# Four-block vision tower: fifth passes of the experts' first layer in row halves, and the second layer in parts between groups of four tiles

## The reference, cut to what matters

```python
h = tok_ref(x)                          # patches to 8 x 64 tokens of 192, a ViT block
h = _layernorm(h + _L0_attn_ref(h))     # 4 experts of windowed attention, gated
h = _layernorm(h + _L0_ffn_ref(h))      # 8 experts, 192 -> 768 -> 192: here
h = _layernorm(h + _L1_attn_ref(h))
h = _layernorm(h + _L1_ffn_ref(h))      # m0: 192 -> 768 -> 192, and class experts: here

def _L0_ffn_ref(x, ...):
    ...
    topv, topi = jax.lax.top_k(probs, 2)
    comb = jnp.sum(topv[..., None] * one_hot(topi, E), axis=2)
    h = gelu(einsum('bnd,edf->bnef', x, w1) + b1)
    y = einsum('bnef,efd->bned', h, w2) + b2
    ffn_out = einsum('bne,bned->bnd', comb, y)
    return ffn_out + bk_scale * spec_out      # spec_out: two recurrences over 64 tokens
```

## Time and profile before

| | us |
|---|---|
| runs | 402.53, 399.41, 400.3 |
| median | 400.3 |
| profiled execution | 399.92 |
| its span (first to last instruction) | 398.2 |
| TensorE busy with matmuls in the span | 377.0 |
| VectorE, ScalarE, GpSimd busy | 242.2, 172.5, 69.3 |

### The profile page before, as it was taken

One profiled execution on the slowest core, in us unless ns is written; L12 is line 12 of the kernel. 1 busy time (PEld: TensorE's weight loads), 2 busy tenths in 40 slices (PEclk: granted clock), 3 DMA queues, 4 the chain that ended last, 5 costly groups with the idle time before them and its releaser, 6 DMA issues.

```text
span 398.2 us, 8780 instructions
## 1 busy us (share of the span) xinstructions
PE 377.0 (95%) x3602; PEld 310.4 (78%) x3602; DVE 242.2 (61%) x712; ACT 172.5 (43%) x302; POOL 69.3 (17%) x113
## 2 busy tenths in 40 slices
PE   8999899999899899989999899999999999999993
PEld 7988779779567575676577698899899898788783
DVE  1567756813299897996364577557658208676443
ACT  1255543471455666644524806325324411541420
POOL 7140010430013231432010400000000200304003
PEclk9999999999999999999999999999999999989999
DMA  8999900000249600000008984404411000000001
GB/s 198 263 203 211 193 17 2 1 2 0 50 124 299 160 2 2 3 2 2 2 0 211 267 210 128 137 10 132 140 21 39 2 0 2 2 2 2 0 2 40
DMA packets 28725, 30.69 MB, mean 77 GB/s; under 512 B 4867, under 2 KB 24137, under 8 KB 28686
## 3 DMA queue, kind: packets, MB, share of 16 engines
q1 hardware_dynamic: 28220, 29.96, 30.4%
q10 hardware_dynamic: 306, 0.17, 0.2%
q0 software_dynamic: 160, 0.01, 0.0%
HBM read 29.73 MB, written 0.39 MB: 76 GB/s over the span
## 4 chain that ended last, share of the span: by engine, by line
PE 62%; DVE 16%; issue 6%; SPq 5%; DMA 5%; ACT 3%; POOL 2%; DVEq 0%; POOLq 0%
PE ps L1533 57%; PE ps L1537 4%; SPq L360 4%; DMA wide<-in_w 3%; DVE front L1204 2%; DMA front<-in_x 2%; DVE front L1193 2%; DVE front L1182 1%; POOL rstd L529 1%; DVE bn L1034 1%; PE ps L1545 1%; DVE front L1194 1%; DVE xn L1049 1%; DVE front L1184 1%; DVE front L1205 1%
## 5 line engine op out<-in xcount | busy, mean ns | idle before, releaser
L1533 PE MATMUL ps<-halves 128*128 128x512 f32 (+2 forms) x380 | 84.4, 376 | 1.7 <-ACT front L747 1.7
L1533 PEld LDWEIGHTS ps<-halves 128*128 128x128 f32 x380 | 66.4, 188 | 14.2 <-ACT front L747 2.6
L1533 PE MATMUL ps<-wide,front 128*128 128x192 f32 x432 | 72.0, 327 | 0.0
L1533 PEld LDWEIGHTS ps<-wide,front 128*128 128x128 f32 x432 | 70.4, 190 | 1.0 <-issue 0.5
L1533 PEld LDWEIGHTS ps<-front 64*32 64x32 f32 (+3 forms) x1488 | 51.4, 132 | 20.5 <-issue 9.4
L1533 PE MATMUL ps<-front 64*32 64x64 f32 (+3 forms) x1488 | 60.0, 241 | 5.8 <-issue 2.3
L747 ACT ACTIVATE front<-ps,colc 128x512 f32<-128x512 f32 x60 | 39.6, 690 | 52.5 <-PE ps L1533 52.4
L573 POOL TENSOR_TENSOR front<-front 128x768 f32<-128x768 f32 x16 | 23.6, 1473 | 71.9 <-DVE front L1205 71.9
L1336 DVE SCALAR_TENSOR_TENSOR xn<-ps,small,xn 128x192 f32<-128x192 f32 x28 | 9.7, 409 | 28.8 <-PE ps L1533 28.8
L1194 DVE TENSOR_TENSOR front<-front 128x768 f32<-128x768 f32 x16 | 24.0, 1502 | 0.5
L1533 PE MATMUL ps<-xT,turned 128*64 128x256 f32 (+1 forms) x96 | 22.6, 458 | 1.4 <-ACT front L785 1.4
(11 more groups left out here) (280 smaller groups left out, 549.8 us busy)
## 6 DMA issues: line engine op xcount, KB each, us to landing
wide<-in_w SPq DMA_DIRECT2D x8, 576.0 KB, 5.4
wide<-in_w SPq DMA_DIRECT2D x8, 384.0 KB, 5.7
wide<-in_w SPq DMA_DIRECT2D x16, 192.0 KB, 6.4
front<-in_a2w SPq DMA_DIRECT2D x5, 576.0 KB
front<-in_a1w SPq DMA_DIRECT2D x5, 384.0 KB
front<-in_x SPq DMA_DIRECT2D x3, 512.0 KB, 7.7
front<-in_w_qkv SPq DMA_DIRECT2D x2, 576.0 KB, 7.4
front<-in_a1w SPq DMA_DIRECT2D x5, 192.0 KB
```

Of the source, the lines that this page charges most:

```text
L1533: return pe.matmul(o, l, r, start=start, stop=stop)
```

## The change

`pair_ends` makes the fifth passes of two tiles as two matmuls with 64 rows each: the first in array rows 0 to 63, the second in rows 64 to 127, into another bank. For that the odd tiles of an expert's weights (and of the feed-forward and m0 weights, which use the same layout) hold high and low the other way round in `both`: `ends_low` subtracts in rows 64 to 127 for even tiles and in rows 0 to 63 for odd ones, two instructions for one. `up_group` takes a group of tiles, makes the four full passes of each, and then the ends in pairs. `up_rest` makes its ends in pairs too. The feed-forward layer of the first block and the last two m0 tiles keep `up` and the five full passes.

The loop over the experts is written anew: three groups of two, then groups of four that may reach over two experts, and between them two or three token tiles of a second layer. `combT` is copied by VectorE ahead of the first `weighted`.

```diff
+            def ends_low(w, raw_w):
+                def turns(v):
+                    return v.rearrange("p (f y n) -> p f y n", y=2, n=P)
+                for y, r in enumerate((slice(DB, P), slice(0, DB))):
+                    ins = dve.tensor_tensor(turns(w.both)[r, :, y], turns(raw_w)[r, :, y],
+                                            turns(w.both.bitcast(F32))[r, :, y], ALU.subtract)
+                return ins
...
-                dve.tensor_tensor(w.both[DB:P], w1s[DB:P, e % NSLOT, 1], w.both[DB:P].bitcast(F32),
-                                  ALU.subtract).then_inc(s["w1_lo"], 1)
+                ends_low(w, w1s[:, e % NSLOT, 1]).then_inc(s["w1_lo"], 1)
...
+            def pair_ends(o, w, n, x, g=None, w2=None):
+                at = slice(0, x.lowB.shape[1]) if g is None else half(g)
+                first = mm(o[0], w.both[0:DB, n[0]], x.lowB[0:DB, at], False, True)
+                return first, mm(o[1], (w2 or w).both[DB:P, n[1]], x.lowB[DB:P, at], False, True)
...
+            def up_group(x, parts):
+                n = [slice(f * P, (f + 1) * P) for w, f in parts]
+                o = [ps[:, (jobs[0] + k) % 4, :] for k in range(len(parts))]
+                for k, (w, f) in enumerate(parts):
+                    pe.wait_ge(s["h_act"], jobs[0] + k - 3)
+                    pe.wait_ge(s["w1_lo"], (jobs[0] + k) // NF)
+                    mm(o[k], w.high[:, n[k]], x.high, True, False)
+                    mm(o[k], w.low[:, n[k]], x.high, False, False)
+                    mm(o[k], w.both[:, n[k]], x.both, False, False)
+                    mm(o[k], w.high[:, n[k]], x.low, False, False)
+                for k in range(0, len(parts), 2):
+                    for ins in pair_ends(o[k:k + 2], parts[k][0], n[k:k + 2], x, w2=parts[k + 1][0]):
+                        ins.then_inc(s["h_mm"], 1)
+                jobs[0] += len(parts)
...
-                for f in range(4):
-                    ins = low_half(ps[:, (jobs[0] + f) % 4, half(g)], w, slice(f * P, (f + 1) * P), x, g)
-                    if g == 1:
-                        ins.then_inc(s["h_mm"], 1)
+                for f0 in (0, 2):
+                    n = [slice(f * P, (f + 1) * P) for f in (f0, f0 + 1)]
+                    o = [ps[:, (jobs[0] + f) % 4, half(g)] for f in (f0, f0 + 1)]
+                    for k in range(2):
+                        mm(o[k], w.high[:, n[k]], x.low[:, half(g)], False, False)
+                    for ins in pair_ends(o, w, n, x, g):
+                        if g == 1:
+                            ins.then_inc(s["h_mm"], 1)
...
+            def up_of(first, n):
+                up_group(xs, [(w1x[u // NF % 2], u % NF) for u in range(first, first + n)])
...
+            for u in range(4, 10, 2):
+                up_of(u, 2)
+            pe.wait_ge(s["comb_done"], 1)
+            for i in range(NT):
+                ins = tr(ps[0:EM, 6, i * P:(i + 1) * P], comb[:, i, :])
+            ins.then_inc(s["combT_mm"], 1)
+            down_of(0, range(3))
+            for e in range(1, EM - 1, 2):
+                up_of(NF * e + 4, 4)
+                down_of(e - 1, range(3, NT))
+                down_of(e, range(2))
+                up_of(NF * (e + 1) + 2, 4)
+                down_of(e, range(2, NT))
+                down_of(e + 1, range(1))
+                up_of(NF * (e + 2), 4)
+                down_of(e + 1, range(1, 3))
...
+            up_of(NF * EM - 2, 2)
+            down_of(EM - 2, range(3, NT))
+            down_of(EM - 1, range(NT))
```

More of the change, by code:

```diff
@@ L978, in weights_low @@
                 dve.wait_ge(s["wx_hi"], n)
-                dve.tensor_tensor(w.both[DB:P], raw_w[DB:P, 1, 0:k], w.both[DB:P].bitcast(F32),
-                                  ALU.subtract).then_inc(s["wx_lo"], 1)
+                if k == MLP:
+                    ins = ends_low(w, raw_w[:, 1, 0:k])
+                else:
+                    ins = dve.tensor_tensor(w.both[DB:P], raw_w[DB:P, 1, 0:k], w.both[DB:P].bitcast(F32), ALU.subtract)
+                ins.then_inc(s["wx_lo"], 1)
             def tokens_low(x, n):
@@ L1013, in weights_split @@
                 dve.tensor_tensor(w.low, raw_w[:, 0, 0:k], w.high.bitcast(F32), ALU.subtract)
-                dve.tensor_tensor(w.both[DB:P], raw_w[DB:P, 1, 0:k], w.both[DB:P].bitcast(F32),
-                                  ALU.subtract).then_inc(s["wx_lo"], 1)
+                ends_low(w, raw_w[:, 1, 0:k]).then_inc(s["wx_lo"], 1)
             def heads_low(g, cols, name):
@@ L1348, in _ @@
                     break
+                if e == 0:
+                    dve.wait_ge(s["combT_mm"], 1)
+                    dve.tensor_copy(combT[0:EM], ps[0:EM, 6, :]).then_inc(s["combT_done"], 1)
                 dve.wait_ge(s["y_mm"], e + 1)
@@ L1353, in _ @@
                 dve.wait_ge(s["y_done"], e + 1)
-                if e == 0:
-                    dve.wait_ge(s["combT_mm"], 1)
-                    dve.tensor_copy(combT[0:EM], ps[0:EM, 6, :]).then_inc(s["combT_done"], 1)
                 for n in range(FIRST + PER * e, min(S, FIRST + PER * (e + 1))):
@@ L1820, in _, with up @@
             jobs = [0]
-            def up(w, x, tiles=range(NF), turn=0, hi="xs_hi", lo="xs_lo"):
+            def up_group(x, parts):
[12 more added lines that the diff above has]
+                jobs[0] += len(parts)
+            def up(w, x, tiles, turn=0):
                 for f in tiles:
@@ L1827, in up @@
                     split_product(ps[:, jobs[0] % 4, :], w, slice(f * P, (f + 1) * P), x,
-                                  turn if f == 0 else 0, hi, lo).then_inc(s["h_mm"], 1)
+                                  turn if f == 0 else 0, "part_hi", "part_lo").then_inc(s["h_mm"], 1)
                     jobs[0] += 1
@@ L1862, in down @@
                         ins.then_inc(s["y_half"], 1)
-                if not halves and not each:
+                if not halves and not each and NT - 1 in tiles:
                     ins.then_inc(s["y_mm"], 1)
@@ L1867, in _ @@
             pe.wait_ge(s["wx_lo"], 3)
-            up(wffx, xs0, range(2), nth(2), "part_hi", "part_lo")
+            up(wffx, xs0, range(2), nth(2))
             pe.wait_ge(s["wt_act"], 2)
@@ L2078, in gates @@
                 ins.then_inc(s["lg_mm"], 1)
[L2080 to L2107, removed]
@@ L2108, in _, with down_of @@
+            def up_of(first, n):
+                up_group(xs, [(w1x[u // NF % 2], u % NF) for u in range(first, first + n)])
+            def down_of(d, tiles):
+                if tiles[0] == 0:
+                    if d >= 2:
+                        pe.wait_ge(s["y_done"], d - 1)
+                    if d == 1:
+                        pe.wait_ge(s["combT_done"], 1)
                     if d == EM - 1:
                         pe.wait_ge(s["extra_done"], 1)
-                    if d == 1:
-                        pe.wait_ge(s["combT_done"], 1)
@@ L2112, in _ @@
-                    if d >= 2:
-                        pe.wait_ge(s["y_done"], d - 1)
                     pe.wait_ge(s["h_act"], NF * (d + 2))
                     pe.wait_ge(w2_in[d % NSLOT], 16 * (d // NSLOT + 1))
-                    down(hT[:, d % 2], w2s[:, d % NSLOT], 4 + 2 * (d % 2), halves=d == EM - 1)
+                down(hT[:, d % 2], w2s[:, d % NSLOT], 4 + 2 * (d % 2), halves=d == EM - 1, tiles=tiles)
+            pe.wait_ge(s["w1_lo"], 1)
+            up_high(w1x[0], xs, 0, nth(4, 0))
@@ new lines, in _ @@
+            up_rest(w1x[0], xs, 0, nth(4, 0))
+            turn_part(xn, 1, 3, (4, 5))
+            keep_busy(2, 6)
+            up_high(w1x[0], xs, 1, nth(4, 1))
+            up_rest(w1x[0], xs, 1, nth(4, 1))
+            part_ready(nth(4, 1))
+            gates()
+            for u in range(4, 10, 2):
[4 more added lines that the diff above has]
+            ins.then_inc(s["combT_mm"], 1)
@@ new lines, in _ @@
+            down_of(0, range(3))
[8 more added lines that the diff above has]
+                down_of(e + 1, range(1, 3))
+            pe.wait_ge(s["chF_in"], 32)
+            pe.wait_ge(s["y_done"], EM - 2)
+            for i in range(NT):
+                mm(two_t(6, i), combT[0:EM, i * P:(i + 1) * P], b2m[0:EM], True, False)
+                ins = mm(two_t(6, i), frow[:, i * P:(i + 1) * P], ow3[0:3], False, True)
@@ L2117, in _ @@
+            ins.then_inc(s["extra_mm"], 1)
+            up_of(NF * EM - 2, 2)
+            down_of(EM - 2, range(3, NT))
+            down_of(EM - 1, range(NT))
             turn_part(xn, 0, 4, (6, 5))
```

## The result

| | before | after |
|---|---|---|
| median | 399.99 us (15 runs, 397.95 to 402.53) | 403.03 us (15 runs, 401.21 to 405.95) |
| ratio, 95% interval | | 1.0089, 1.0063 to 1.0115 |
| profiled execution, its span | 399.92, 398.2 us | 405.95, 404.1 us |
| TensorE busy, granted clock over the span | 377.0 us, 0.995 | 380.4 us, 0.987 |

The profiled execution after is the slowest of its 15, 6.0 us over the one before, where the medians are 3.0 apart. So the two traces must be compared stage by stage, and what belongs to one execution taken out.

The account below looks back on a forecast made before the run. TensorE was taken to bound the kernel from 241.91 us to the experts' end. +1.37 us there and +0.92 for m0 made +2.3 on the profiled 399.92: 402.2 us, with an 8 in 10 range of 397.9 to 404.9.

Parts of the forecast that it names:

- the clock's rival: After the longer wait for comb the clock falls, halving 3.41 us of second layer: +1.7, 403.9 us; chance 0.13.
- step 1: Fifth passes in row halves: the halves overlap, a pair saving 0.232 us (512 columns) or 0.12 (256).
- The rival of turns: The two halves of each pair run one after the other: +5.1 us on top, 407.3 us; chance 0.07.
- The round trip, 0.40: TensorE's switch from full passes to row halves and back costs 0.40 us; a group of four gains 0.06.
- The rival of weights loaded ahead: Weight loads hide under 512-column passes, a round trip costs 0.19: -1.4 us, 398.5 us; chance 0.11.
- Expert 0 and m0, 0.92 each: Four half-width pairs each in expert 0 and the last layer's m0 weights: 3 x 0.28 + 0.08 = +0.92 us apiece.
- step 2: Start of the experts: late activations delay comb, TensorE waits 2.3 us instead of 1.26, two tiles still owed: +2.14 us.
- step 3: Steady part of the experts: eight groups of four give 0.48 back, tiles 46-47 take 0.17, the 0.46 wait goes.
- The sum: +1.37 us to the end of the experts and +0.92 for m0, together +2.3 us: 402.2 us.

Follow-up runs that it names:

- the kernel that takes turns: The changed kernel with both ends of every pair on array rows 0 to 63, so they can't run side by side: 408.31 us, 1.0205.
- the order alone: The changed kernel's new order of tiles and parts, with every fifth pass at full height again: 402.19 us, 1.0042.
- two by two: The changed kernel with each group of four made as two groups of two: 406.94 us, 1.0172.
- the old order: The kernel before, its layer order kept, with row halves in one group of four for each of experts 1 to 7: 399.18 us, 0.998.
- busy through the wait: The changed kernel with nine idle-filling transposes of the identity in the wait for comb: 402.36 us, 1.0063.

## Why the prediction was right, point by point

Forecast 402.2 us, 0.5% over the median of before; measured 403.03, 0.9%. The mechanism, the sign and most sizes held; the last 0.8 us did not, and the measured time lies halfway between the forecast and the clock's rival (403.9).

- **Overlap (step 1).** Two 64-row matmuls in 0.50 us, against 0.7 in the same rows. The rival of turns was priced at 5.1 us; the kernel that takes turns is 5.3 over the changed one.
- **The round trip, 0.40.** 0.39 from the groups of the order alone, 0.43 from two by two. The rows of another stage, fp32 with 128 columns, were enough to price it. A group of four was to gain 0.06 and gains 0.07. The rival of weights loaded ahead (0.19 for a round trip) fell with this.
- **Expert 0 and m0, 0.92 each.** 0.81 and 0.88. A half-width pair was a little too dear.
- **The start of the experts (step 2).** Counted from the end of the gates (218.61 forecast, 219.75 in this trace), ScalarE was to take tile 4 after 2.57 us and did after 2.56; the exponential was to follow at 5.15 (222.27 + 1.49 - 218.61) and did at 5.15; the transposes were to start at 9.74 and did at 9.77. The wait forecast at 2.3 is 2.24.
- **The steady part (step 3).** No wait between groups, and the old 0.46 gone. From the gates to the end of the experts +0.45 was forecast (1.37 less expert 0's 0.92) and +0.36 came at the full clock.
- **The sum.** 2.3 forecast, 2.05 in the traces at the full clock. The medians are 3.0 apart (2.5 to 4.6 by the interval), about 1 us more than the structure.
- **The clock.** I had kept it as a rival of 0.13 (a fall after the wait of `comb`, +1.7). In the profiled execution that fall came as the rival said and cost 1.7, and a second one came where I had none, after the matmuls of 8 and 3 rows, which in the trace of before passed at the full clock; it cost 1.5.

Whether the clock makes the 1 us between the medians is not shown. The mean granted clock over the timed runs is 0.9885 for the changed kernel (15 runs) and 0.9887 for the kernel before (51 runs timed beside the experiments, without that of 403.26 us). By the estimate above that is about 2.7 falls a run in either. So the trace of before, with one fall and a granted clock of 0.995, is not a typical run of it. It could be that falls cost less where before has them: half clock costs 0.5 us in the attention and 1.5 to 1.7 in the experts. Against that stands that in both kernels the runs at a lower clock are the longer ones, and by a straight line through the timed runs a fall's worth of clock goes with about 1.2 us more in either. Only the profiled runs have a trace, so where the falls of the others lie is not known, and this part of the difference stays open.

What makes the clock fall after the matmuls of 8 and 3 rows stays open too. It does within 1.1 us of the end of the last of them in seven of the ten traces, and not in those of before, of the old order and of busy through the wait. In the first two a second layer follows these matmuls, elsewhere two tiles of a first layer; but busy through the wait has them between the same rows as the changed kernel. No run was made to tell this apart.

## What to carry to other kernels

Two matmuls of half the rows run side by side, but a switch into that form and back costs about 0.4 us of TensorE here, nearly two passes of 512 columns: gather as many halves as there are banks before switching, and don't use it for two tiles or for half-width passes. When a new order moves the operand of a serial chain on other engines behind more TensorE work, follow that chain to the place where TensorE asks for its result, and move the asking too: that gave 3.7 us here, where the halves in groups of four gave 1.1 at most over the same order without them. Price a clock fall by the stage that it hits.

## What the runs showed of the hardware that was not expected

- The round trip costs the same with 512 columns in fp32r as with 128 in fp32: 0.39 to 0.43 us, of which 0.09 is the late start of the first pair (0.32 for 0.232), 0.10 each lies between the pairs and behind the second (0.34 and 0.33), and 0.10 is paid in the row behind the group.
- TensorE fell to the lower clock, 0.5 for 3.41 us, while it was busy the whole time: 2.90 us of the 2.90 from 324.90 with matmuls of 8 and 3 rows, then 1.1 us of full passes at the full clock, then the fall at 328.98.
- A pause of 2.24 us was followed by a fall in two traces, pauses of 1.62, 2.06 and 2.48 (twice) in none.
- The granted clock differs between executions of one kernel: 0.983 to 0.993 over the changed kernel's 15 timed runs.
